# A new hand-written order of steps for a two-block attention and expert kernel on one core

## The reference

```python
x = x + tanh(g_xattn[0]) * attention(layernorm(x), ctx)     # 16 heads of 64
x = x + tanh(g_ffn[0])   * experts(layernorm(x))            # 8 dense experts, softmax gate, threshold 0.1
x = x + tanh(g_xattn[1]) * attention(layernorm(x), ctx)     # 16 heads of 16
x = x + tanh(g_ffn[1])   * routed_experts(layernorm(x))     # 8 experts, SwiGLU; the first 512 tokens
```

## Time and profile before

| what | value |
|---|---|
| median of 3 runs | 3772.34 us (3772.3 to 3773.69) |
| profiled execution | 3774.71 us |
| its span, first to last instruction | 3772.6 us |
| mean granted TensorE clock | 0.996 of full |
| busy share PE, PE weight loads | 97%, 79% |
| busy share DVE, ACT, POOL | 70%, 45%, 37% |
| chain that ended last | PE 91%, DVE 6%, ACT 1%, issue 1% |

### The profile page before, as it was taken

The page is one execution under the profiler, slowest core; times in us unless marked ns, Lnnn a source line. Parts: engine busy times, 40 slices in busy tenths (PEclk is TensorE's granted clock), DMA queues, the critical chain, the costliest instruction groups (busy, mean ns, idle before and its releaser), DMA issues.

```text
span 3772.6 us, 95482 instructions
## 1 busy us (share of the span) xinstructions
...
## 2 busy tenths in 40 slices
...
GB/s 96 11 14 16 12 12 16 12 12 16 12 12 16 12 12 16 12 13 16 12 13 16 11 13 16 12 13 16 12 13 16 11 13 16 11 13 16 11 26 65
DMA packets 58916, 64.83 MB, mean 17 GB/s; under 512 B 5344, under 2 KB 55808, under 8 KB 58240
## 3 DMA queue, kind: packets, MB, share of 16 engines
...
...
## 4 chain that ended last, share of the span: by engine, by line
PE 91%; DVE 6%; ACT 1%; issue 1%; POOL 0%; SPq 0%; DMA 0%; DVEq 0%; ACTq 0%; POOLq 0%
PE g L818 28%; PE g L824 17%; PE scores L818 12%; PE scores L921 6%; PE g L971 6%; DVE xn L1177 4%; PE g L887 4%; PE g L990 3%; PE scores L955 3%; PE scores L981 3%; PE g L838 3%; PE scores L925 2%; PE g L898 1%; DVE kT_lo L1207 1%; ACT kT_hi L663 1%
## 5 line engine op out<-in xcount | busy, mean ns | idle before, releaser
L761 ACT ACTIVATE prob<-scores 120x1024 f32<-120x1024 f32 x512 | 498.5, 1023 | 509.0 <-PE scores L925 438.4
L1316 DVE SCALAR_TENSOR_TENSOR x<-g,lg_w,x 128x256 f32<-128x256 f32 x1024 | 494.8, 483 | 250.3 <-PE g L818 226.7
L597 POOL TENSOR_TENSOR q_lo<-an,q_hi 128x512 fp32r<-128x512 f32 x256 | 331.7, 1308 | 278.0 <-ACT q_hi L790 278.0
L818 PE MATMUL g<-ew_hi,yT_hi 128*128 128x512 f32 x1024 | 426.5, 416 | 0.0
L818 PE MATMUL g<-ew_lo,yT_hi 128*128 128x512 f32 x1024 | 401.7, 392 | 0.0
L818 PE MATMUL g<-ew_hi,yT_lo 128*128 128x512 f32 x1024 | 399.5, 390 | 0.0
L1255 DVE TENSOR_REDUCE y_nm<-g 128x4 f32<-128x480 f32 x512 | 301.0, 650 | 110.6 <-PE g L898 110.6
L542 POOL TENSOR_TENSOR y_rstd<-y_mv,eps 128x2 f32<-128x2 f32 x128 | 25.0, 195 | 960.7 <-DVE y_mv L1172 960.7
L1255 DVE TENSOR_REDUCE x_nm<-g 128x4 f32<-128x480 f32 x512 | 313.1, 654 | 82.6 <-PE g L887 82.6
L592 POOL TENSOR_TENSOR q_lo<-q_full,q_hi 128x512 fp32r<-128x512 f32 x256 | 330.3, 1299 | 65.3 <-ACT q_full L695 65.3
L542 POOL TENSOR_TENSOR x_rstd<-x_mv,eps 128x2 f32<-128x2 f32 x64 | 12.5, 195 | 886.1 <-DVE x_mv L1172 886.1
...
## 6 DMA issues: line engine op xcount, KB each, us to landing
...
ctx_in<-in_ctx ACTq DMA_DIRECT2D x128, 120.0 KB, 2.3
...
```

What stands on the lines that cost most here:

```text
L597: g.tensor_tensor(q[1][:, 2 * h:2 * h + 2, :], an[:, 2 * (h % 2):2 * (h % 2) + 2, :], q[0][:, 2 * h:2 * h + 2, :].bitcast(F32), ALU.subtra ...
L761: a.activation(prob[:, e].rearrange("p o u s -> p (o u s)"), scores[0:NK, banks, :].rearrange("p o c -> p (o c)"), ACT.Exp, scale=scale).t ...
L818: ins = t_.matmul(out_, lhsT[u], rhs[v], start=first and n == 1, stop=last and n == 3 * len(terms))
L1316: ins = v.scalar_tensor_tensor(out=x1[:, t, :], in0=ring.bank(Y_FFN[j])[:, o * D:(o + 1) * D], scalar=lg_w[:, t, 2 * n + o:2 * n + o + 1], ...
```

## The change

No instruction is added, removed or altered. `ORDER` and the lists of iterations -1, 0, 1 and 63 in `ENDS` hold the same pairs in another order; those of iterations 64 and 65 stay. The ring banks follow from the order. This is the loop's list, whole:

```diff
 ORDER = (
-    ("n_load", 0), ("x_st", 0), ("x_st", 1), ("y_ffn", 0), ("n_stat", 0), ("y_ffn", 1), ("z_hi", 1), ("y_k", 0),
-    ("y_ffn", 2), ("y_ffn", 3), ("n_norm", 0), ("y_ffn", 4), ("y_ffn", 5), ("x_st", 2), ("x_st", 3), ("y_ffn", 6),
-    ("n_tr", 0), ("y_ffn", 7), ("y_stat3", 0), ("x_sum", 0), ("x_pv", 0), ("x_mul", 0), ("x_mul", 1), ("x_hi", 0),
-    ("y_norm3", 0), ("x_mul", 2), ("x_mul", 3), ("x_pv", 1), ("x_pv", 2), ("x_hi", 1), ("x_sum", 1), ("x_pv", 3),
-    ("y_tr3", 0), ("z_out", 0), ("x_hi", 2), ("y_v", 0), ("n_ctx", 0), ("y_q", 0), ("x_hi", 3), ("n_k", 0),
-    ("x_out", 0), ("y_max", 0), ("x_out", 1), ("x_out", 2), ("y_max", 1), ("y_res", 0), ("x_out", 3), ("p_stat", 0),
-    ("y_maxt", 0), ("n_q", 0), ("n_k", 1), ("n_q", 1), ("y_maxt", 1), ("p_norm", 0), ("n_q", 2), ("p_load", 0),
-    ("p_tr2", 0), ("n_q", 3), ("n_max", 0), ("y_st", 0), ("n_max", 1), ("p_gate", 0), ("n_v", 0), ("p_lg", 0),
-    ("n_res", 0), ("n_maxt", 0), ("y_st", 1), ("n_max", 2), ("n_v", 1), ("n_max", 3), ("p_wt", 0), ("y_pv", 0),
-    ("y_mul", 0), ("y_pv", 1), ("y_mul", 1), ("n_maxt", 1), ("p_ctx", 0), ("p_eb", 0), ("y_hi", 0),
+    ("n_load", 0), ("x_st", 0), ("x_st", 1), ("y_ffn", 0), ("y_ffn", 1), ("x_st", 2), ("n_stat", 0), ("n_norm", 0),
+    ("x_st", 3), ("y_ffn", 2), ("y_ffn", 3), ("y_ffn", 4), ("n_tr", 0), ("y_ffn", 5), ("y_ffn", 6), ("z_hi", 1),
+    ("y_ffn", 7), ("x_sum", 0), ("y_stat3", 0), ("x_pv", 0), ("x_mul", 0), ("x_pv", 1), ("x_pv", 2), ("x_hi", 0),
+    ("x_hi", 1), ("x_sum", 1), ("x_mul", 1), ("y_norm3", 0), ("x_mul", 2), ("x_pv", 3), ("x_hi", 2), ("x_mul", 3),
+    ("y_k", 0), ("y_tr3", 0), ("z_out", 0), ("x_hi", 3), ("y_v", 0), ("n_ctx", 0), ("y_q", 0), ("n_k", 0), ("x_out", 0),
+    ("y_max", 0), ("y_res", 0), ("x_out", 1), ("p_load", 0), ("x_out", 2), ("y_max", 1), ("x_out", 3), ("n_q", 0),
+    ("y_maxt", 0), ("p_stat", 0), ("n_q", 1), ("y_maxt", 1), ("n_k", 1), ("n_q", 2), ("n_q", 3), ("p_norm", 0),
+    ("n_max", 0), ("p_tr2", 0), ("y_st", 0), ("n_max", 1), ("p_gate", 0), ("n_max", 2), ("n_v", 0), ("p_lg", 0),
+    ("n_maxt", 0), ("y_st", 1), ("n_max", 3), ("n_v", 1), ("n_res", 0), ("p_wt", 0), ("n_maxt", 1), ("y_pv", 0),
+    ("y_mul", 0), ("y_pv", 1), ("p_ctx", 0), ("y_hi", 0), ("p_eb", 0), ("y_mul", 1),
 )
```

More of the change, by code:

```diff
@@ L64 @@
     -1: (
-        ("n_load", 0), ("n_stat", 0), ("n_norm", 0), ("n_ctx", 0), ("n_tr", 0), ("n_k", 0), ("n_k", 1), ("n_q", 0),
-        ("n_q", 1), ("n_q", 2), ("n_q", 3), ("n_max", 0), ("n_max", 1), ("n_v", 0), ("n_v", 1), ("n_res", 0),
-        ("n_max", 2), ("n_maxt", 0), ("n_max", 3), ("n_maxt", 1),
-    ),
-    0: (
[L70 to L76, removed]
-    ),
@@ L78 @@
-    1: (
[L79 to L88, removed]
+        ("n_load", 0), ("n_stat", 0), ("n_norm", 0), ("n_tr", 0), ("n_ctx", 0), ("n_k", 0), ("n_q", 0), ("n_q", 1),
@@ new lines @@
+        ("n_v", 0), ("n_k", 1), ("n_q", 2), ("n_q", 3), ("n_max", 0), ("n_res", 0), ("n_max", 1), ("n_max", 2),
+        ("n_v", 1), ("n_maxt", 0), ("n_max", 3), ("n_maxt", 1),
+    ),
+    0: (
+        ("n_load", 0), ("n_stat", 0), ("x_st", 0), ("x_st", 1), ("n_norm", 0), ("x_st", 2), ("x_st", 3), ("x_pv", 0),
+        ("x_mul", 0), ("x_sum", 0), ("x_pv", 1), ("x_mul", 1), ("x_hi", 0), ("n_ctx", 0), ("x_hi", 1), ("p_load", 0),
+        ("x_mul", 2), ("x_sum", 1), ("x_pv", 2), ("x_pv", 3), ("x_hi", 2), ("x_hi", 3), ("x_mul", 3), ("n_k", 0),
+        ("n_k", 1), ("n_tr", 0), ("x_out", 0), ("n_res", 0), ("x_out", 1), ("x_out", 2), ("x_out", 3), ("p_stat", 0),
+        ("n_q", 0), ("n_q", 1), ("n_q", 2), ("p_norm", 0), ("n_q", 3), ("n_max", 0), ("p_tr2", 0), ("p_gate", 0),
+        ("n_max", 1), ("n_max", 2), ("p_lg", 0), ("n_v", 0), ("n_maxt", 0), ("n_max", 3), ("p_wt", 0), ("n_v", 1),
+        ("p_eb", 0), ("p_ctx", 0), ("n_maxt", 1),
+    ),
@@ new lines @@
+    1: (
+        ("n_load", 0), ("y_ffn", 0), ("y_ffn", 1), ("n_stat", 0), ("y_ffn", 2), ("x_st", 0), ("x_st", 1), ("n_norm", 0),
+        ("y_ffn", 3), ("x_st", 2), ("y_ffn", 4), ("n_tr", 0), ("y_ffn", 5), ("y_ffn", 6), ("y_ffn", 7), ("x_sum", 0),
+        ("y_stat3", 0), ("x_pv", 0), ("x_st", 3), ("x_mul", 0), ("x_hi", 0), ("x_hi", 1), ("x_pv", 1), ("y_norm3", 0),
+        ("x_mul", 1), ("x_sum", 1), ("x_mul", 2), ("x_pv", 2), ("x_mul", 3), ("x_pv", 3), ("x_hi", 2), ("y_tr3", 0),
+        ("y_k", 0), ("x_hi", 3), ("y_v", 0), ("n_ctx", 0), ("n_v", 0), ("y_q", 0), ("n_v", 1), ("x_out", 0),
+        ("y_res", 0), ("y_max", 0), ("x_out", 1), ("x_out", 2), ("y_max", 1), ("x_out", 3), ("n_q", 0), ("n_k", 0),
+        ("p_stat", 0), ("n_k", 1), ("y_maxt", 0), ("y_maxt", 1), ("n_q", 1), ("n_q", 2), ("n_res", 0), ("p_norm", 0),
+        ("n_q", 3), ("n_max", 0), ("p_tr2", 0), ("n_max", 1), ("p_load", 0), ("y_st", 0), ("n_max", 2), ("p_gate", 0),
+        ("p_lg", 0), ("n_max", 3), ("n_maxt", 0), ("y_st", 1), ("p_wt", 0), ("y_pv", 0), ("y_mul", 0), ("y_pv", 1),
+        ("n_maxt", 1), ("y_mul", 1), ("y_hi", 0), ("p_ctx", 0), ("p_eb", 0),
@@ L89 @@
     ),
     B - 1: (
[L91 to L100, removed]
+        ("m_coef", 0), ("x_st", 0), ("y_ffn", 0), ("y_ffn", 1), ("y_ffn", 2), ("z_hi", 1), ("y_ffn", 3), ("y_ffn", 4),
@@ new lines @@
+        ("y_ffn", 5), ("y_ffn", 6), ("y_ffn", 7), ("x_st", 1), ("m_coef", 1), ("m_load", 0), ("m_zero", 0), ("x_st", 2),
+        ("x_pv", 0), ("m_stat", 0), ("y_stat3", 0), ("x_sum", 0), ("x_mul", 0), ("x_st", 3), ("x_pv", 1), ("x_hi", 0),
+        ("m_coef", 2), ("x_sum", 1), ("x_mul", 1), ("x_pv", 2), ("x_hi", 1), ("m_norm", 0), ("m_coef", 3), ("x_mul", 2),
+        ("x_hi", 2), ("y_norm3", 0), ("x_pv", 3), ("m_tr", 0), ("p_load", 0), ("z_out", 0), ("x_mul", 3), ("y_k", 0),
+        ("y_tr3", 0), ("m_ct", 0), ("x_out", 0), ("x_hi", 3), ("y_q", 0), ("m_tr", 1), ("m_dnb", 0), ("m_bias", 0),
@@ L101 @@
+        ("y_res", 0), ("x_out", 1), ("y_max", 0), ("x_out", 2), ("p_ctx", 0), ("y_max", 1), ("x_out", 3), ("p_stat", 0),
+        ("m_gu", 0), ("p_norm", 0), ("y_maxt", 0), ("y_v", 0), ("p_tr2", 0), ("y_maxt", 1), ("p_gate", 0), ("y_st", 0),
+        ("p_lg", 0), ("m_gu", 1), ("y_st", 1), ("y_mul", 0), ("y_pv", 0), ("p_wt", 0), ("y_pv", 1), ("y_hi", 0),
+        ("p_eb", 0), ("y_mul", 1),
     ),
```

## The result

The changed kernel takes 3801.43 us, median of 4 (3797.03 to 3802.21), against 3772.32 (3771.96 to 3773.69) for the kernel before, 4 runs too. The ratio is 1.0074, 95% interval 1.0057 to 1.0092: 29 us slower, where 55 us faster was forecast. The profiled execution has a span of 3799.7 us at a granted clock of 0.997.

The account below looks back on a forecast made before the run. PE, 98% busy, was taken as the bound. Per iteration 0.62 + 0 + 0.13 + 0.26 - 0.10 = 0.91 us, times 61 is 55.5, giving 3717 us; range 3688 to 3764.

Parts of the forecast that it names:

- (a): PE's stall at p_tr2 behind the normalising pair: 0.88 us an iteration falls to 0.26, gain 0.62, the main term.
- Two waits in place of one: Rival: second instruction of p_norm and y_norm3 misses the moment between POOL's low parts, waits 1.3 longer; 3833, chance 0.08.
- Strict turns: Rival: POOL and DVE alternate by whole instructions at the port, POOL's copy starts 0.4 later; 3753, chance 0.2.
- (b): PE's stall of 0.17 at y_tr3 behind y_norm3: goes, but turns into a wait at y_q; net 0.
- (c): PE's stall of 0.13 at y_pv 0, whose bank ACT empties: goes, as DVE empties its new bank earlier; gain 0.13.
- (d): PE's stall of 0.26 at the next x_st 0, waiting for n_maxt 1's copy: goes, gain 0.26.
- the price of n_maxt 1: n_maxt 1 now waits for n_max 3's two reductions on DVE: costs 0.10 us an iteration, between 0 and 0.3.
- all four stalls go: Rival: all 1.44 us of stall an iteration vanish, needing POOL clear of p_norm; 3684, chance 0.05.
- The ends: Iterations -1, 0 and 63, outside the 61 loop iterations: nothing expected on balance, 4 us either way.

Follow-up runs that it names:

- run 4: The changed kernel with p_norm ahead of n_k 1, which moves it on DVE alone; 3787.89 us, ratio 1.0044.
- run 5: The changed kernel with p_stat ahead of n_q 0 and p_norm ahead of n_k 1; 3707.79 us, ratio 0.983.
- run 7: The changed kernel with the order edits of run 5 and the cut POOL instructions of run 6 together; 3706.93 us, ratio 0.9829.
- run 1: The changed kernel with the loop's stretch between x_out 3 and y_st 0 put back as before, except p_load; 3772.67 us, ratio 1.0002.
- run 9: The changed kernel with only POOL's low part of n_q cut in two, the masked copy whole; 3741.98 us, ratio 0.9914.
- run 10: The changed kernel with POOL made to wait, before n_q 1's low part, for ACT's high part of n_k 1; 3774.12 us, ratio 1.0.
- run 2: The kernel before with only the stretch from p_load to n_max 0 ordered as in the change; 3812.23 us, ratio 1.011.
- run 3: The changed kernel with p_stat ahead of n_q 0 again, so POOL makes the root before the low part; 3799.03 us, ratio 1.0071.
- run 11: The change in the loop's list alone, with the lists in ENDS (iterations -1, 0, 1 and 63) in the old order; 3821.37 us, ratio 1.0137.
- run 6: The changed kernel, order untouched, with POOL's masked copy of n_k cut into four and its low part of n_q into two; 3707.62 us, ratio 0.9831.
- run 8: The kernel before, order untouched, with POOL's masked copy cut in four and low part of n_q in two; 3714.9 us, ratio 0.9843.

## Why the prediction was wrong

The periods below are the distance between the loads of iterations 2 and 62, divided by 60. "DVE to POOL" is the start of the pair less the start of POOL's masked copy; it is negative where DVE asked first. Both and the length of the pair are from the timelines of one iteration; in the 58 to 60 iterations between 200 and 3550 us neither moves by more than 0.02 in any of these kernels. Runs 4, 5 and 7 are left out, since their pair meets the low parts and not the copy first.

| kernel | median us | period | DVE to POOL | pair |
|---|---|---|---|---|
| before | 3772.32 | 56.60 | -0.32 | 2.31 |
| run 1, old stretch | 3772.67 | 56.39 | -0.33 | 2.31 |
| run 9, low part cut | 3741.98 | 56.05 | -0.29 | 2.27 |
| run 10, POOL waits | 3774.12 | 56.56 | -0.80 | 2.79 |
| after | 3801.43 | 57.00 | -0.01 | 3.22 |
| run 2, new stretch | 3812.23 | 57.12 | -0.01 | 3.21 |
| run 3, root early | 3799.03 | 57.02 | -0.03 | 3.25 |
| run 11, old ends | 3821.37 | 56.97 | -0.01 | 3.22 |
| run 6, all cut | 3707.62 | 55.49 | -0.29 | 1.07 |
| run 8, all cut, old order | 3714.9 | 55.69 | -0.47 | 1.25 |

**The step that failed** is in (a): "So both arrive together, as they do now", and from it "I take the same pattern again". They did not arrive together before. There the copy starts at 1600.34, and the timelines of DVE and POOL have the pair 0.32 ahead of it, while the low part still runs. The prediction has this number ("with POOL busy for the first 0.32 or so") and yet calls it together:

```profile
1600.02 2.31 DVE L1177 TENSOR_SCALAR xn<-x,y_mv,y_rstd 128x256 f32<-128x256 f32 x2
...
1599.09 1.29 POOL L592 TENSOR_TENSOR q_lo<-q_full,q_hi 128x512 fp32r<-128x512 f32 x1
```

DVE asks while the low part runs, and goes at its end. My own two numbers for the change, DVE at 41.6 to 41.7 and the copy at 41.75, left a tenth, less than had been seen to be enough. DVE came at 41.54. POOL came at 41.55, 0.2 earlier than computed: the root was done at 40.33 (1608.49), not at about 40.5, and a low part costs 1.25 from start to start (1608.46 to 1609.71), not 1.31. The margin went from 0.32 to 0.01, and the pattern flipped: two POOL instructions waited out in place of one. I priced the pattern and not the margin that it hangs on; a tenth or less in an arrival became 1.0 us in the end of xn.

**The size.** Forecast stall 0.26, measured 1.45: 1.19 more. Of this, 1.03 is xn, done at 44.77 on the clock instead of 43.74; 0.16 is PE, which asks at 43.44 instead of 43.6 and loses nothing by that. (With the prediction's own 41.70 and 1.94 PE asks at 43.64, and the forecast stall would be 0.22.) So p_tr2 starts 1.03 late, 63 us in 61 iterations. Behind p_tr2 an iteration takes 0.26 more than forecast, 16 us. With the ends (3.6) and 2 us more (the profiled execution stood 2.4 above the median before and stands 0.4 above it now), that is the 84 us between forecast and result.

**The rivals.** "Two waits in place of one" had the mechanism, at chance 0.08: it said that if DVE misses the moment between two POOL instructions it waits 1.3 longer. It looked for this at the second instruction of the pair; the one that misses is the first. At p_norm the size came near, 1.19 of stall. At y_norm3 it did not: the pair there still takes 1.70, and its part of that rival's price is missing. So 3833 was too high. "Strict turns" is wrong in its forecast: in run 9, where DVE's first goes ahead, the copy starts as the low part ends and is 0.04 longer (1.83 against 1.79), not 0.4 later. But the rule of the page that it rested on stands well: the Trainium skill, SBUF — State Buffer, section Who interferes with whom, has the port pair as an exclusive lock for a whole instruction. Here each normalising instruction that lost ended 0.15 to 0.17 us after the end of a POOL instruction of 1.3 to 1.8 us. The prediction held the first one's 0.52 us in the kernel before against the rule, and misread it: the low part ends at 1600.38, the instruction at 1600.54, 0.16 later, like those that lost. The page's other sentence, that issue order decides, is not settled here. In the change DVE's first instruction is recorded 0.01 ahead of the copy and loses, but its record also begins 0.08 before DVE's previous one ends (1609.78), so the records do not say who asked first.

**The rest of the sum** holds to a tenth, as two misses cancel. (b) went slightly better: y_q starts at 25.13 on the clock, against 25.3 forecast and 25.27 before, and the wait of 0.3 forecast there did not come. That is the 0.16 by which PE is early at p_tr2. (c), (d) and the price of n_maxt 1: from p_wt's transposes to x_st 0 it was 3.20 us and is 2.90 (1622.21 to 1625.11), a gain of 0.30 for the forecast 0.29. Not counted was that n_max 2, n_v 0, n_v 1 and n_max 3 in new neighbourhoods take 4.61 us from start to start in place of 4.43 in PE's timeline: 0.18 of the 0.26 above. Forecast period 55.7 plus 1.19 is 56.9; measured 57.0. Run 9, where the pattern held (with low parts 0.14 longer), has 56.05. Run 6, with no wait at p_tr2, has 55.49, and the forecast without its 0.26 has 55.43. So "all four stalls go" at 3684 was out of reach in this order.

**The ends** cost 3.6 us net, within the 4 us given: 1.5 less before the loop, 5.1 more behind iteration 63. Of these, 2.6 are one wait of PE for DVE's x at L1316, which the kernel before does not have: y_mul 1 is now the last step of iteration 63, and the chain there runs through its instructions on DVE into L1316. The other 2.5 were not followed.

**What the range missed.** The prediction said that it would be wrong "if the period is above 56.4, if p_norm lasts well over 2.4 us": both came. The case of two waits was left outside the range, although the only evidence against it was today's pattern, which the change was moving.

**Is there a better version?** Runs 5, 6 and 7 beat both kernels, at 3707.79, 3707.62 and 3706.93 us, 1.7% below the kernel before. Cutting looks like the sturdier cure: in runs 6, 8 and 7, where the pair meets POOL at three different moments, it takes 1.07, 1.25 and 1.56 us. That a margin of a tenth would then cost at most one piece is argued, not run.
